# Attention stages of a graph network: maxima kept at most 16 units ahead instead of 20, and a head's shift row stored from the middle of the head before

## The reference, cut to what matters

```python
e = jax.nn.leaky_relu(as_n[src] + ad_n[dst], NEG_SLOPE)
m = jax.ops.segment_max(e, dst, num_segments=N)
p = jnp.exp(e - m[dst])
s = jax.ops.segment_sum(p, dst, num_segments=N)
alpha = p / (s[dst] + 1e-16)
out = jax.ops.segment_sum(alpha[:, :, None] * h[src], dst, num_segments=N)
```

## Time and profile before

| | us |
|---|---|
| median of 3 runs (lowest to highest) | 3948.47 (3946.04 to 3948.95) |
| the profiled execution: device time | 3976.25 |
| the profiled execution: span | 3974.7 |
| wide attention, first to last `weigh` (L1129) | 623.7 to 1094.8 |
| narrow attention, first to last `weigh` (L1129) | 1657.1 to 2049.3 |

### The profile page before, as it was taken

The page is one execution under the profiler, slowest core; times in us unless marked ns, Lnnn a source line. Parts: engine busy times, 40 slices in busy tenths (PEclk is TensorE's granted clock), DMA queues, the critical chain, the costliest instruction groups (busy, mean ns, idle before and its releaser), DMA issues.

```text
span 3974.7 us, 58219 instructions
## 1 busy us (share of the span) xinstructions
PE 3632.0 (91%) x18463; PEld 2974.8 (75%) x18473; DVE 1958.0 (49%) x2783; ACT 1682.1 (42%) x2911; POOL 1556.0 (39%) x1168
## 2 busy tenths in 40 slices
PE   8998868999988897599989999999999999979998
PEld 4555437999978897333336999999999999945588
DVE  7245788888543635899955332233333320022234
ACT  1113687888823321499961333333333333300021
POOL 3888886666500001000002444444444444366600
PEclk9999998999989998799999999999999999999999
DMA  4343112222233302211124555555555553288801
GB/s 144 94 117 74 45 23 64 85 82 86 65 109 103 115 28 88 101 40 40 33 86 135 192 178 185 182 189 182 185 180 172 180 185 111 95 285 269 250 14 69
DMA packets 176461, 483.10 MB, mean 122 GB/s; under 512 B 40799, under 2 KB 57206, under 8 KB 176343
## 3 DMA queue, kind: packets, MB, share of 16 engines
q1 hardware_dynamic: 87414, 201.95, 15.7%
q0 software_dynamic: 54368, 185.24, 15.4%
q10 hardware_dynamic: 34560, 94.45, 6.7%
HBM read 357.64 MB, written 123.55 MB: 121 GB/s over the span
## 4 chain that ended last, share of the span: by engine, by line
PE 44%; ACT 7%; DVE 3%; issue 2%; another core or an unknown queue 1%; DMA 0%; DVEq 0%; SPq 0%; POOL 0%; ACTq 0%; POOLq 0%
PE ps L1894 30%; PE ps L1988 4%; ACT work L1279 3%; PE ps L1882 3%; ACT ps L1270 3%; PE ps L1558 3%; PE ps L306 2%; PE ps L298 1%; DVE work L1101 1%; PE ps L1216 1%; DVE hbuf L2011 0%; DVE work L1129 0%; ACT work L1289 0%; DMA ct<-x_d 0%
## 5 line engine op out<-in xcount | busy, mean ns | idle before, releaser
L1894 PE MATMUL ps<-wsplit,xsplit 128*128 x6840 | 1238.4, 337 | 2.7 <-DVEq L1834 2.7
L1894 PEld LDWEIGHTS ps<-wsplit,xsplit 128*128 128x128 f32 x6840 | 1182.9, 188 | 2.9 <-issue 2.9
L1831 DVE CAST wsplit<-wplain 128x768 fp32r<-128x768 f32 x204 | 117.4, 575 | 760.8 <-PE ps L1894 745.4
L1861 POOL TENSOR_TENSOR xsplit<-ct,xsplit 128x768 fp32r<-128x768 f32 x190 | 369.3, 1943 | 296.6 <-ACTq L1926 296.5
L1279 ACT ACTIVATE work<-ps,work 128x418 f32<-128x418 f32 x720 | 437.7, 631 | 108.9 <-PE ps L1189 100.0
L1931 ACT ACTIVATE ct<-ps,invs 128x768 f32<-128x768 f32 x190 | 171.4, 902 | 714.5 <-PE ps L1894 714.5
L1226 PE MATMUL ps<-hbuf,work 128*128 128x193 f32 x2400 | 455.9, 328 | 14.7 <-DVE work L1143 13.1
L1226 PEld LDWEIGHTS ps<-hbuf,work 128*128 128x128 f32 x2400 | 408.1, 190 | 42.7 <-issue 18.3
L1270 ACT ACTIVATE ps<-work,lr 128x418 f32<-128x418 f32 x720 | 431.6, 634 | 6.0 <-DMA work<-lrow_d 6.0
L1129 DVE SCALAR_TENSOR_TENSOR work<-work,cnt 128x1250 f32<-128x1250 f32 x240 | 350.1, 1459 | 133.1 <-ACT work L1279 79.3
L1856 POOL DMA_INDIRECT ct<-x_d,relrec x190 | 200.6, 1056 | 457.9 <-PE ps L1882 450.4
(11 more groups left out here) (212 smaller groups left out, 4201.9 us busy)
## 6 DMA issues: line engine op xcount, KB each, us to landing
wplain<-in_L_gnn_W_rel SPq DMA_DIRECT2D x34, 2304.0 KB
msg_d<-ct ACTq DMA_DIRECT2D x190, 384.0 KB, 2.6
work<-lrow_d SPq DMA_DIRECT2D x47, 625.0 KB
feat_d<-work ACTq DMA_DIRECT2D x30, 386.0 KB
hbuf<-feat_d SPq DMA_DIRECT2D x60, 193.0 KB
gat_d<-work POOLq DMA_DIRECT2D x12, 960.0 KB
xplain<-gat_d SPq DMA_DIRECT2D x30, 384.0 KB
work<-xa_d SPq DMA_DIRECT2D x27, 384.0 KB
```

The costliest lines, as they stand in the source:

```text
L1861: g.tensor_tensor(xlo7[:, k % XW, :], xt7[:, k % 2].rearrange("p c n -> p (c n)"), xhi7[:, k % XW, :].bitcast(F32), ALU.subtract).then_inc ...
L1894: last = pe.matmul(ps[:, 4 + 2 * (u % 2) + h, 0:HALF], x[:, u, c * P:(c + 1) * P], w[:, bass.ds(base + (c * D + h * HALF), HALF)], start=( ...
```

## The change

The bound on the maxima becomes q + 1 + NT + LEAD with LEAD = 6, sixteen units ahead. Units 0 and 1 have two maxima, all others up to unit 103 have one. The tenth maximum of head h comes in unit 10(h - 1) + 3 (unit 3 of the head in front), and with it `shifts(h)`. `evict` stays where it is. On SP, `shift(h + 1)` stands inside head h, after the features that wait for unit 10h + 3, instead of `shift(h + 2)` at its end; `l_row(h + 3)` follows it, without its own wait for unit 10h + 1; `shift(1)` is no longer ahead of the loop.

```diff
-            AHEAD = 4
+            AHEAD, LEAD = 4, 6
...
                 shift(0)
                 l_row(2)
-                shift(1)
                 for h in range(H):
+
 
                     if h + 1 < H:
                         r_row(h + 1)
-                    unit_done(NT * h + 1)
-                    if h + 3 < H:
-                        l_row(h + 3)
-                    if h + 2 < H and not self.narrow:
-                        for k in range(5):
+                    for k in range(5):
+                        if k == 2 and h + 1 < H:
+                            shift(h + 1)
+                        if k == 3 and h + 3 < H:
+                            l_row(h + 3)
+                        if h + 2 < H and not self.narrow:
                             unit_done(NT * h + 2 + k)
                             features(h + 2, 2 * k, 2 * k + 2)
-                    if h + 2 < H:
-                        shift(h + 2)
...
                 late = 3 if self.narrow else 0
                 for q in range(NT * H):
                     weigh(q)
-                    upto = min(taken + 2, q + 1 + 2 * NT)
+                    upto = min(taken + 2, q + 1 + NT + self.LEAD)
                     for t in range(taken, upto):
                         maximum(t)
                     taken = upto
```

## The result

| | before | after |
|---|---|---|
| median | 3948.71 us (3946.04 to 3950.26, 4 runs) | 3971.91 us (3967.54 to 3974.77, 4 runs) |
| ratio after / before | | 1.0058, 95% interval 1.0046 to 1.007 |
| PE, first to last sum of the wide attention | 475.7 us (625.3 to 1100.9) | 471.9 us (624.5 to 1096.4) |
| PE, first to last sum of the narrow attention | 394.2 us (1658.6 to 2052.8) | 423.3 us (1652.1 to 2075.4) |

What follows compares the result with a forecast made beforehand. PE was taken to bound the wide attention and ACT the narrow one, DVE mattering only where its work bunches. -5.9 + 21.4 + 11.9 - 2.3 = +25.1 on 3948.5 gave 3973.6 us, range 3959 to 3981.

Steps and rivals of the forecast that it cites:

- rival A: The forecast itself: shifts and evict meet in the narrow attention and PE's clock falls; +25.1 us, 3973.6, chance 0.66.
- The give of 0.65 us: Narrow attention's loop: a `weigh` may be 0.65 us late for free; anything beyond delays ACT and is never made up.
- rival B: Narrow attention: the meeting of shifts and evict costs DVE time but PE's clock stays up; +13.2 us, 3961.7, chance 0.20.
- Part 1: Start of the narrow attention: units 2 to 5 lose one maximum each, so unit 9 comes earlier; 5.9 us gained.
- Part 2: Narrow attention: shifts and evict meet in unit 3 ten times, DVE needing 6.23 us for that unit; 21.4 us lost.
- Part 3: Narrow attention: PE's gap grows to 3.19 us and its clock falls nine times in ten, 1.3 each; 11.9 us lost.
- Part 4: Wide attention: one maximum in units 2 to 5 keeps DVE ahead in the first head; 2.3 us gained, nothing later.
- 0.54 + 3 x 0.59: Wide attention's first head: PE's idle before unit 3 plus three intervals of 4.41 instead of 3.82; 2.3 us gained.
- Part 5: SP's transfers in both attentions: the new order of shift stores, features and L rows brings neither gain nor loss.
- Rival C: Narrow attention: ACT makes up a single `weigh` 3.15 us late, leaving only the gains; -8.2 us, 3940.3, chance 0.04.
- D: All ten clock falls, longer or at full 1.52 us, or wide unit 3 costs: +28 to +33, up to 3981, chance 0.06.
- E: Evict or shifts partly covered unseen, or the change does less than it says: within 8 us of before, chance 0.04.

Runs made afterwards that it cites:

- experiment 2: Changed kernel with five extra matmuls that nothing reads filling part of PE's gap in the narrow attention: 3962.53 us, 1.0034 of before.
- experiment 7: The changed kernel itself measured once more, without edits, as reference on the second chip: 3971.90 us, 1.0059 of before.
- Experiment 1: Changed kernel with the narrow evict in unit 6 of the next head instead of unit 3: 3952.81 us, 1.0006 of before.
- experiment 3: Changed kernel, sixteen ahead in the wide attention only: 3948.09 us, ratio 0.9994; then twenty in both, leaving only SP's order: 3950.28 us, 1.0002.
- experiment 6: Changed kernel, narrow lead growing from 14 to 19 by extra maxima in units 0, 7, 10, 18, 27, evict in unit 5: 3941.01 us, ratio 0.9983.
- experiments 5: Changed kernel, maxima twenty ahead in both attentions, narrow evict moved to unit 9 to meet the shifts there: 3973.61 us, 1.0064 of before.

## Why the prediction was right

3973.6 was predicted, 3971.9 measured, within the range, and rival A is what happened. By its steps:

- **The give of 0.65 us.** Right, and exact: heads of 34.5 without the fall of the clock, as rival B had worked out, seen in experiment 2 and in the first heads of experiment 7. Experiment 1 shows it for a second lateness: 1.78 late, 1.1 lost.
- **Part 1, the start of the narrow attention.** Unit 4 was to start at 16.43 behind unit 0 and starts at 16.43 (1650.61 to 1667.04). Unit 9 was to come 31.18 behind; adding the measured intervals, it comes at 31.16 (1681.77), which is 5.9 earlier than before.
- **Part 2, the meeting.** Predicted 6.23, measured 6.20; PE's gap 3.19 against 3.15.
- **Part 3, the clock.** The choice between A and B was the doubtful one and came out for A. Ten falls in the profile of after, seven in that of experiment 7, where nine were assumed; 1.38 each where 1.3 was taken (the 11.9 is nine times 1.32, which is 1.52 less 0.2). The spare of 0.2 that I subtracted from 1.52 is about what the runs show.
- **Part 4, the wide attention.** The mechanism was right, the size not: 2.3 predicted, 3.8 in the profile of after and 2.8 to 4.0 in the seven profiles with sixteen in the wide one. The term that was mis-sized is "0.54 + 3 x 0.59". It adds up PE's idle time before units 3 to 6 in one profile and takes PE's slow first unit as given. In the seven profiles that first unit takes 5.2 us (experiment 3, where the clock rises 4.3 behind the first `weigh`) to 6.4 (experiment 6, 6.8 behind it), and all the rest of the stretch takes 466.5 in each: with sixteen PE sets the pace from the start, and what it wins in its first unit stays won. With twenty ahead DVE sets the pace of the first six units, and a faster start of PE wins nothing: the stretch is 475.6 or 475.7 with a first unit of 5.2, 6.4 or 6.5. For before's own first unit, 6.5, the gain would be 2.7, an estimate (475.7 less 466.5 and 6.5); the rest of the 3.8 is the clock's earlier rise. That nothing changes later was right: from unit 10 on the wide attention takes 431.0 in every profile, before and after.
- **Part 5, SP.** Right: experiment 3 has the order of SP alone, and nothing moved.

Taken together, for the profile of after: -5.9 + 21.4 + 13.8 - 3.8 = +25.5, where its attentions show +25.3. The medians show 23.2. That the forecast came within 2 us of the measured time is partly luck: against this profile part 3 was 1.9 too low and part 4 left out a gain of 1.5, and the two nearly cancel. Nor could the number of falls be known beforehand, since the same kernel shows ten in one profile and seven in the other.

Rival C (a single late `weigh` is made up) fell with the first heads of 34.5. Rivals D and E fell with the result itself, though all ten falls, which D counts on, did happen in the profile of after. Experiment 1, which changes one constant and takes the loss back, shows that it was the meeting.

## What to carry to other kernels

In a loop over three engines, measure how late one engine may be before the next loses time, and where another engine's own extra work covers it. Two periodic pieces of work on one engine should not share an iteration, and a piece that was free in its old place may not be so in a new one: here the shifts were covered by ACT's copies in units 9 and 0, cost 1.1 us a head in unit 3, and 2.1 with the evict in the same unit. Then look at the gap this leaves on TensorE: if it is near one behind which the clock fell, expect a fall in most rounds (26 of 29 here).

## What the runs showed of the hardware

I had not expected that one and the same gap, 3.14 us in the same loop of one execution, leaves the granted clock at 1.00 in three heads and is followed by the 1.2 GHz level in the seven after them. In the profiles of after and of experiments 5 and 7 there are 29 gaps of 3.12 to 3.16 in heads with a meeting, and 26 falls. In experiment 7 a fall costs a head 1.3 to 1.4 us. In experiment 2, 2.3 us of matmuls that nobody reads keep the clock up. The gaps of 1.06 and 1.76 never led to one in the steady heads. How the chip chooses between the two outcomes at 3.14 is left open here.
